# Loads on one queue, B first, and W1 of the first batch ahead on VectorE

## The reference, cut to what matters

```python
# x (8, 512, 256), cond (8, 8); all float32
masked_w = weight * mask[None]                      # weight (8, 256, 256), mask (256, 256)
w_bot    = einsum('bg,got->bot', cond, masked_w)    # one 256x256 matrix for each batch
x        = x + einsum('bnt,bot->bno', x, w_bot) + bias

base = einsum('btc,oc->bto', x, W_base) + b_base
h    = einsum('btc,erc->bter', x, As)               # As (8, 16, 256)
lora = einsum('bter,eor,be->bto', h, Bs, cond)      # Bs (8, 256, 16)
x    = x + base + lora * 2.0
```

## Time and profile before

| | us |
|---|---|
| median of 3 runs | 56.79 (56.75 to 57.19) |
| the profiled execution | 56.88 |
| its span in the profile | 55.1 |
| busy: TensorE, VectorE, ScalarE, GpSimd | 50.7, 39.5, 31.7, 31.5 |

### The profile page before, as it was taken

One profiled execution on the slowest core, in us unless ns is written; L12 is line 12 of the kernel. 1 busy time (PEld: TensorE's weight loads), 2 busy tenths in 40 slices (PEclk: granted clock), 3 DMA queues, 4 the chain that ended last, 5 costly groups with the idle time before them and its releaser, 6 DMA issues.

```text
span 55.1 us, 972 instructions
## 1 busy us (share of the span) xinstructions
PE 50.7 (92%) x330; PEld 45.6 (83%) x330; DVE 39.5 (72%) x64; ACT 31.7 (58%) x53; POOL 31.5 (57%) x30
## 2 busy tenths in 40 slices
PE   2998999699999999999999999999999999999900
PEld 2988999699998978998898889889889889888800
DVE  0049999989596975999999988689929809805030
ACT  1939900447809499619705992992992950850800
POOL 4003400199990098999995999999999910000000
PEclk9999999999999999999999999999999999999999
DMA  0599999999999995000630072063054054059582
GB/s 0 136 377 313 363 390 400 426 401 426 425 384 413 416 396 208 15 0 0 253 134 0 12 272 109 0 241 146 0 223 158 0 205 176 0 196 372 193 286 95
DMA packets 5477, 11.79 MB, mean 214 GB/s; under 512 B 609, under 2 KB 1377, under 8 KB 5473
## 3 DMA queue, kind: packets, MB, share of 16 engines
q1 hardware_dynamic: 5184, 11.35, 54.7%
q10 hardware_dynamic: 288, 0.39, 2.1%
HBM read 7.54 MB, written 4.19 MB: 213 GB/s over the span
## 4 chain that ended last, share of the span: by engine, by line
PE 77%; DVE 11%; DMA 5%; issue 2%; DVEq 0%
PE ps_out L457 13%; PE ps_out L461 13%; PE ps_out L465 13%; PE ps_merge L457 7%; PE ps_merge L461 7%; PE ps_merge L465 7%; DVE B_lo L324 7%; PE ps_out L527 6%; DMA lora_sb<-factors_A_dram 5%; PE ps_lora L457 3%; PE ps_lora L461 3%; PE ps_lora L465 3%; DVE W L330 1%; DVE out_sb L448 1%; DVE A_lo L389 1%
## 5 line engine op out<-in xcount | busy, mean ns | idle before, releaser
L191 POOL TENSOR_TENSOR W_lo<-W,W_hi 128x512 fp32r<-128x512 f32 x8 | 13.3, 1657 | 5.3 <-ACT W_hi L240 5.3
L358 DVE TENSOR_TENSOR x_lo<-x_sb,x_hi 128x1024 fp32r<-128x1024 f32 x8 | 11.9, 1485 | 0.2 <-ACT x_hi L260 0.2
L457 PE MATMUL ps_out<-x_hi,M_hi 128*128 128x512 f32 (+1 forms) x32 | 9.8, 388 | 0.0
L461 PE MATMUL ps_out<-x_lo,M_hi 128*128 128x512 f32 (+1 forms) x32 | 9.7, 384 | 0.0
L465 PE MATMUL ps_out<-x_hi,M_lo 128*128 128x512 f32 (+1 forms) x32 | 9.7, 383 | 0.0
L253 ACT ACTIVATE M_hi<-ps_merge 128x512 fp32r<-128x512 f32 x8 | 4.8, 595 | 7.6 <-PE ps_merge L465 7.6
L197 POOL TENSOR_TENSOR W_lo<-W,W_hi 128x512 fp32r<-128x512 f32 x6 | 8.8, 1459 | 0.3 <-ACT W_hi L246 0.3
L260 ACT ACTIVATE x_hi<-x_sb 128x1024 fp32r<-128x1024 f32 x8 | 8.4, 1055 | 0.0
L240 ACT ACTIVATE W_hi<-W 128x512 fp32r<-128x512 f32 x8 | 5.0, 629 | 5.9 <-DVE W L330 3.6
L373 DVE TENSOR_SCALAR out_sb<-ps_out,bias_sb 128x512 f32<-128x512 f32 x7 | 5.2, 747 | 4.1 <-PE ps_out L465 4.0
L201 POOL TENSOR_TENSOR W<-W,ident 128x256 f32<-128x256 f32 x6 | 6.4, 1071 | 2.9 <-DVE x_lo L358 2.9
(11 more groups left out here) (58 smaller groups left out, 71.4 us busy)
## 6 DMA issues: line engine op xcount, KB each, us to landing
x_sb<-xT_dram SPq DMA_DIRECT2D x8, 512.0 KB, 10.5
outT_dram<-out_sb SPq DMA_DIRECT2D x15, 256.0 KB, 2.3
packs_sb<-packs_dram SPq DMA_DIRECT2D x7, 288.0 KB, 5.4
rows_sb<-rows_dram SPq DMA_DIRECT2D x1, 384.0 KB, 7.1
base_sb<-base_dram ACTq DMA_DIRECT2D x1, 256.0 KB, 3.6
outT_dram<-out_sb SPq DMA_DIRECT2D x2, 128.0 KB, 1.8
packs_sb<-head_dram SPq DMA_DIRECT2D x1, 192.0 KB, 3.5
packs_sb<-rest_dram SPq DMA_DIRECT2D x1, 160.0 KB, 3.9
```

What stands on the lines that cost most here:

```text
L191: pool.tensor_tensor(W1_lo[:, b % W1BUF], W1[:, b % W1BUF], W1_hi[:, b % W1BUF].bitcast(f32), ALU.subtract).then_inc(w1lo_done, 1)
L358: nc.vector.tensor_tensor(x_lo[:, b % XBUF], x_sb[:, b], x_hi[:, b % XBUF].bitcast(f32), ALU.subtract).then_inc(xlo_done, 1)
L457: nc.tensor.matmul(out, hi_l, hi_r, start=(n == 0), stop=False)
L461: nc.tensor.matmul(out, hi_l, lo_r, start=False, stop=False)
```

## The change

SyncE's queue issues all loads: `factors_B`, which now holds the condition and B, then `factors_A` (biases and A), `head`, `rest`, `base`, and then the packs. ScalarE issues none, and its `b_hi` waits for B alone. On VectorE, `w1(0)` follows `b_lo(0)` to `b_lo(3)`, then `b_lo(4)`, `b_lo(5)`, and the `w0` and `w1` that follow; `b_lo(6)` stands ahead of `ramp_low(0)`, `b_lo(7)` ahead of `m_lo(0)`, and `bias_sum` behind `low_bias`. On TensorE one product less is done on zeros, and in `lora_first` the second hi x hi product comes ahead of the wait for `A_lo`.

```diff
--- before.py
+++ after.py
@@ -32,10 +32,10 @@
     SINGLE = 4
     XBUF = 4
     W1BUF = 4
-    WARM = 28
+    WARM = 27
     assert packs.shape == (NQ - 1, P, PACKW)
 
-    OB0, OB1, OA, OBT = NB, NB + NT, NB + 2 * NT, NB + 2 * NT + C
+    OBT, OB0, OB1, OA = NB, NB + C, NB + C + NT, NB + C + 2 * NT
     cut = MIXW + C
 
     with ExitStack() as ctx:
@@ -58,7 +58,7 @@
             return (packs_sb[:, at:at + EXPW].rearrange("p (k c) -> p k c", k=KQ),
                     packs_sb[:, at + EXPW:at + PACKW].rearrange("p (j t) -> p j t", j=NT))
 
-        lora_sb = sb("lora_sb", [P, OBT + C])
+        lora_sb = sb("lora_sb", [P, OA + C])
         cond_er = lora_sb[:, 0:NB]
         bias0 = lora_sb[:, OB0:OB0 + NT]
         bias1 = lora_sb[:, OB1:OB1 + NT]
@@ -143,9 +143,11 @@
 
         @block.sync
         def _(sp):
-            sp.dma_start(lora_sb[:, 0:OBT], factors_A).then_inc(lora_arrived, 16)
+            sp.dma_start(lora_sb[:, 0:OB0], factors_B).then_inc(B_arrived, 16)
+            sp.dma_start(lora_sb[:, OB0:OA + C], factors_A).then_inc(lora_arrived, 16)
             sp.dma_start(packs_sb[:, 0:cut], head).then_inc(mix_in, 16)
             sp.dma_start(packs_sb[:, cut:MIXW + PACKW], rest).then_inc(pack_in[0], 16)
+            sp.dma_start(base_sb[:, :, :], base.rearrange("p (j o) -> p j o", j=NT)).then_inc(base_in, 16)
             for q in range(1, NQ):
                 at = MIXW + q * PACKW
                 sp.dma_start(packs_sb[:, at:at + PACKW], packs[q - 1]).then_inc(pack_in[q], 16)
@@ -269,14 +271,11 @@
                 nc.scalar.activation(out_sb[:, b % 2, 0, :], ps_out[b % 2 * NT][:, :], ACT.Identity,
                                      bias=bias_sb[:, 0, b:b + 1]).then_inc(out_done[0], 1)
 
-            act.dma_start(lora_sb[:, OBT:OBT + C], factors_B).then_inc(B_arrived, 16)
 
             act.wait_ge(warm_set, 1)
             nc.scalar.activation(table_sb[:, :], warm[:, 0:1], ACT.Copy)
-            act.dma_start(base_sb[:, :, :], base.rearrange("p (j o) -> p j o", j=NT)).then_inc(base_in, 16)
 
             act.wait_ge(B_arrived, 16)
-            act.wait_ge(lora_arrived, 16)
             for b in range(NB):
                 b_hi(b)
             w1_hi(0)
@@ -389,16 +388,17 @@
             nc.vector.scalar_tensor_tensor(out=A_lo[:, :], in0=A_er, scalar=SCALING, in1=A_hi[:, :].bitcast(f32),
                                            op0=ALU.mult, op1=ALU.subtract).then_inc(alo_done, 1)
             dve.wait_ge(B_arrived, 16)
-            for b in range(NB):
+            for b in range(4):
                 b_lo(b)
-            nc.vector.tensor_tensor(bias_sum[:, :], bias0, bias1, ALU.add).then_inc(fixed_done, 1)
-            dve.wait_ge(fixed_done, 1)
+
+            dve.wait_ge(base_done, NT)
+            w1(0)
+            b_lo(4)
+            b_lo(5)
             w0(0)
             w0(1)
-            dve.wait_ge(base_done, NT)
-            w1(0)
+            w1(1)
             w0(2)
-            w1(1)
             w0(3)
             w0(4)
             w1(2)
@@ -409,9 +409,11 @@
             dve.wait_ge(w0_done, NQ)
             nc.vector.tensor_tensor(W0[:, 0:2, 1, H:C], W0[:, 0:2, 1, H:C], ident[:, :].unsqueeze(1).to_broadcast([P, 2, P]),
                                     ALU.add).then_inc(eye_second, 1)
+            b_lo(6)
             ramp_low(0)
             ramp_low(1)
             split_x_lo(0)
+            b_lo(7)
             m_lo(0)
 
             dve.wait_ge(row_done, 1)
@@ -421,6 +423,7 @@
             nc.vector.tensor_scalar(low_bias[:, :], cond_er, A_bias0[:, :], SCALING,
                                     ALU.mult, ALU.mult).then_inc(low_done, 1)
 
+            nc.vector.tensor_tensor(bias_sum[:, :], bias0, bias1, ALU.add).then_inc(fixed_done, 1)
             m_lo(1)
             split_x_lo(1)
 
@@ -429,6 +432,7 @@
                 dve.wait_ge(dots_done, 1 + j)
                 dot(base_rows[:, j, :], base_bias0[:, j:j + 1]).then_inc(dots_done, 1)
             dve.wait_ge(dots_done, 1 + NT)
+            dve.wait_ge(fixed_done, 1)
             for j in range(NT):
                 last = nc.vector.tensor_scalar(bias_sb[:, j, :], ps_bias[:, j, :], base_bias0[:, j:j + 1],
                                                bias_sum[:, j:j + 1], ALU.add, ALU.add)
@@ -474,10 +478,10 @@
                 pe.wait_ge(ahi_done, 1)
                 pe.wait_ge(bhi_done, 1)
                 term(0, 0, A_hi, B_hi, first=True)
+                pe.wait_ge(bhi_done, 2)
+                term(1, 0, A_hi, B_hi, first=True)
                 pe.wait_ge(alo_done, 1)
                 term(0, 0, A_lo, B_hi)
-                pe.wait_ge(bhi_done, 2)
-                term(1, 0, A_hi, B_hi, first=True)
                 term(1, 0, A_lo, B_hi)
                 pe.wait_ge(blo_done, 1)
                 term(0, 0, A_hi, B_lo, last=True)
@@ -631,8 +635,8 @@
     masks = mask.reshape(NT, P, NQ, TQ).transpose(1, 2, 0, 3).reshape(P, NQ, NT * TQ)
     packs = np.concatenate([mix.reshape(P, P), np.concatenate([experts, masks], axis=2).reshape(P, -1)], axis=1)
     A_er = As.reshape(G * R, C)
-    lora = np.concatenate([np.repeat(cond.T, R, axis=0), halves(bias0[:, None]), halves(bias1[:, None]),
-                           A_er, Bs.transpose(0, 2, 1).reshape(G * R, C)], axis=1)
+    lora = np.concatenate([np.repeat(cond.T, R, axis=0), Bs.transpose(0, 2, 1).reshape(G * R, C),
+                           halves(bias0[:, None]), halves(bias1[:, None]), A_er], axis=1)
 
     rows = np.concatenate([halves(base), np.broadcast_to(bias0, (P, C))], axis=1)
     xT = np.ascontiguousarray(x.transpose(0, 2, 1).reshape(NB, NT, P, TOK).transpose(0, 2, 1, 3).reshape(NB, P, NT * TOK))
@@ -640,7 +644,7 @@
     first = P + packs.shape[1] // NQ - P // NQ
     arrays = {"head": packs[:, :cut], "rest": packs[:, cut:first],
               "packs": packs[:, first:].reshape(P, NQ - 1, -1).transpose(1, 0, 2), 
-              "factors_A": lora[:, :-C], "factors_B": lora[:, -C:], "base": halves(base.T), "rows": rows, "xT": xT}
+              "factors_A": lora[:, NB + C:], "factors_B": lora[:, :NB + C], "base": halves(base.T), "rows": rows, "xT": xT}
     arrays = {n: np.ascontiguousarray(a) for n, a in arrays.items()}
 
     nc = bacc.Bacc("TRN2", target_bir_lowering=False, num_devices=1)
```

## The result

| | before | changed |
|---|---|---|
| median us | 56.79 (56.75 to 57.19, 4 runs) | 57.85 (57.43 to 58.22, 4 runs) |
| ratio, 95% interval | | 1.0167 (1.0129 to 1.0205): slower by over 1% |
| profiled execution, its span | 56.88, 55.1 | 57.94, 56.1 |

Ratios leave out executions that are over 1.5% above the fastest of the same kernel; medians do not, so where a kernel scatters widely its median says less of a gain, or more of a loss, than its ratio.

The account below looks back on a forecast made before the run. TensorE was taken as the bound, with 0.70 us idle ahead of `lora(2)`. Gain 0.70 + 0.05 - max(0.15 for A, 0.2 for packs) = 0.55, within base's limit 0.65; 56.79 - 0.55 = 56.24, say 56.25; range 55.95 to 56.90.

Parts of the forecast that it names:

- What bounds the kernel: TensorE, without a break from 10.15 to 52.35; only 0.70 us idle ahead of `lora(2)`, waiting for `W1(0)`, can be won.
- The order's worth, 0.70 + 0.05: TensorE's front: 0.70 us from an earlier `W1(0)`, 0.05 from an earlier product with `B_lo`.
- A, d = 0.15: Load of A, lands 0.15 us later on the single queue, between bounds of 0 and 0.44.
- The packs, e = 0.2, at most 0.9: First pack's load ahead of `mixed(1)`, lands 0.2 us later, between bounds of 0 and 0.9.
- the first sign that the prediction names for its being wrong: TensorE waiting at `mixed(1)` for a pack, listed first of three signs against the forecast.
- A backlog of bytes and not of issues: Packs' loads: seven packs' median latency 5.4 against the first's 4.6, read as bytes limiting; the reason for taking 0.2.
- my high bound: First pack's load: issued at 3.0, it again takes 4.6 us to land, so it comes 0.9 later.
- the room of 0.14: At `mixed(1)`: the first pack landed at 6.71 before, and `mixed(1)` started at 6.85.
- Rival 2: At `mixed(1)`: first pack 0.9 later, 0.75 to 0.8 wait, 56.8 to 56.9; chance 0.22 together with the mild late base.
- Base, L = 5.74: Base's landing time, 4.82 before, bounds 5.54 and 7.1; the chain to `ramp_first` allows a gain of 6.39 - L = 0.65.
- The rule weighed: Merging the load queues can only give back saved issue time; 0.44 charged to A makes 56.48, none 56.04.
- L + 1.35: VectorE's start of `W1(0)`, 7.1: base's landing L, GpSimd beginning 0.19 later and taking 1.14 for two halves.

Follow-up runs that it names:

- e1_order: The kernel before with only VectorE's new order, its loads staying on two queues: 56.61 us, ratio 0.9947.
- e14: e1_order repeated unaltered, in five rounds: 56.75 us, ratio 0.9940.
- e5: The kernel before with 27 instead of 28 products on zeros, nothing else: 56.87 us, ratio 1.0010.
- e4: The changed kernel with 28 instead of 27 products on zeros: 57.50 us, ratio 1.0103.
- e11: The changed kernel once more, unaltered, for a second trace: 57.65 us, ratio 1.0162.
- e16: The changed kernel with 28 products on zeros again, in five rounds: 57.56 us, ratio 1.0125.
- e17: The changed kernel unaltered, run beside e16 on the same chip: 57.59 us, ratio 1.0118.
- e6: e1_order with two small loads, read by nobody, issued by SyncE ahead of the packs: 56.80 us, ratio 0.9971.
- e8: The changed kernel with 28 products on zeros, B (and the condition) and base issued by ScalarE's queue as before: 56.90 us, ratio 0.9977.
- e15: The changed kernel with 28 products on zeros and base alone on ScalarE's queue, issued at 2.26 after the table's activation: 56.78 us, ratio 0.9959.
- e7: The changed kernel with 28 products on zeros and A, B, condition and biases in one load on the single queue: 57.41 us, ratio 1.0080.
- e13: e1_order with base issued by ScalarE only once B has landed, at 3.6: 59.88 us, ratio 1.0541.
- e2: The changed kernel with VectorE's order of before, the loads staying on one queue: 57.54 us, ratio 1.0069.
- e9: The changed kernel with 28 products on zeros and B alone on ScalarE's queue: 57.04 us, ratio 1.0022.
- e10: The changed kernel with 28 products on zeros, one queue, base issued behind the first pack: 58.62 us, ratio 1.0294.
- e12: The changed kernel with 28 products on zeros and the first pack issued by ScalarE's queue once B has landed: 58.62 us, ratio 1.0290.
- e3: The changed kernel with base alone issued by ScalarE's queue from the start; its trace issued base ahead of A: 58.15 us, ratio 1.0064, inconclusive.
- e18: e1_order with 30 products on zeros: 56.59 us, ratio 0.9929.

## Why the prediction was wrong

- **What bounds the kernel:** right. The 0.70 of idle time was there for `W1(0)`, the new order removes it (9.48 in e1_order against 9.45), and no work behind it loses the gain.
- **The order's worth, 0.70 + 0.05:** right in one trace (0.66), less than half of it in the rest, 0.3 by the ratios and 0.13 to 0.27 by the medians. I read a pause of one traced execution as pure waste. It covered two things that vary from run to run: the start of the faster products (e14) and a late pack (e5). How much of the missing gain each takes, no run shows.
- **A, d = 0.15:** too much. A landed at 1.17 + 2.2 = 3.37, 0.13 earlier than before, and the first product started at 3.81 instead of 4.36. Nothing came of it: the products ran at 0.21 us, and `mixed(1)` had to wait anyway.
- **The packs, e = 0.2, at most 0.9:** this is the step that failed. e was 8.44 - 6.71 = 1.73 in the changed kernel's trace and 1.1 to 1.9 in those of e4, e11, e16 and e17, where `mixed(1)` started at 7.8 to 8.7. TensorE's wait there is the first sign that the prediction names for its being wrong. "A backlog of bytes and not of issues" gave the later issue almost no price and took for granted that the bytes move at the rate of before. In the traces the issue's 0.95 came through whole; and the bytes moved at 201 to 258 GB/s (291 in e11) instead of 340 from 3.5 to 5.5, so that the latency, which my high bound held at 4.6, was 4.7 to 5.6. The sum with the measured term, 0.75 - 1.73 = -0.98, comes near the 1.0 by which the span grew, but partly by luck: it leaves out the room of 0.14, and the 0.05 did not come. Rival 2 named the place, at half of its price.
- **Base, L = 5.74:** also too early, it was 6.58, and 6.7 to 7.2 in the traces of e4, e11, e16 and e17. By my working that allows a gain of -0.2, with the chain as measured (L + 8.84) one of 0.1, and at 7.2 a loss of 0.5. So even with punctual packs the forecast would not have come true. It decided in none of these traces: the first merge did not wait for `ramp_first`. In e4 it was close, `ramp_first` ending at 15.93 and its product starting at 16.09.
- **The rule weighed.** The Trainium skill ("DMA: Bandwidth & Descriptors", section "Issuing engines are not separate DMA queues") says that issuing from several engines only saves the sequencer's issue time. I had weighed the merging of the queues by that: up to 0.44. Here e6 puts the issue time of two loads at 0.15 us, e8 against e4 and e16 puts both together at 0.7 to 0.8, and e15 against e7, with the packs issued at one time, puts the second queue at 0.7. The measurement decides, as far as medians go: in this first stretch of small loads the second queue was worth more than its issue time. That the loads share the same engines, which the section also says, fits e13, where base gained nothing from a queue of its own.

**What stays open.** Why the rate falls, and why the medians of e15 and e7 part where their traces don't. In steps of half a microsecond from 2.5 to 6 us the lowest rate is 76 to 155 GB/s in e2, e4, e7, e9, e10, e11, e12, e13 and e17, 202 and 208 in e16 and the changed kernel, and 205 to 329 where base goes out early on ScalarE's queue. A load that is already under way on the second queue goes with the runs where this is mild, but no run shows what the engines wait for then, and its place moves from trace to trace. e8 also lies 0.2 us above e1 and e14 by the ratios; whether the new contents of the loads do that is not shown. The rows of load sizes changed too (B's from 1024 to 1056 bytes, A's from 1072 to 1040); e8 has the new sizes and a rate of 347, so they are not what lowers the rate.

## What to carry to other kernels

An idle time on the critical chain of one trace may be the cushion of a neighbour that varies, here a late load and a late speed-up of TensorE, so don't take the whole of it as the gain until several traces agree; here the runs gave a fifth to a half. Move the order of compute and the queues of the loads in separate steps: one gained 0.6% here (0.9929 to 0.9947 in three runs, one of them with 30 products on zeros) and the other lost 1.3 to 1.5%. "Same bytes ahead" is no price for a load: charge a later issue in full as the high bound, read GB/s in the stretch that the load moves through, and count on another rate when the set of queues at work there changes. And when two traces and two medians disagree, as in e15 and e7, see first where in its own spread each traced execution lies.

## What the runs showed of the hardware that I had not expected

- TensorE's products of 256 columns came every 0.21 us (1.2 columns a ns, as its level of 1.2 GHz would give) or every 0.12 (2.1, near the 2.4 GHz level), while the granted clock of the stretch reads 1.00 in both cases. The change from one to the other lay between 4.4 us and some time past 7.6 (e3), in traces of the same kernel at 4.4 and 6.2 (e1, e14), at 4.8 and at 6.6 or later (e4, e16), with TensorE busy on zeros from 0.98 to 4.15 ahead of it in each of these four. The number of products on zeros, 27 or 28, did not decide it.
- A load of 256 KB issued to an idle second queue at 3.6 us took 6.1 us to land (e13), where one issued at 1.2 took 3.6 to 3.9 (before, e1, e5, e6, e8, e14, e18).
- The two 128 x 128 additions on GpSimd took 1.14 us in all beside VectorE's `b_lo` (1.32 in e14) and 0.87 with VectorE idle. That made `W1(0)` start L + 1.06 where I had worked out L + 1.35.
